# The output projection of a self-attention in three rounded passes, with its weights split on GpSimd

## The chip, the cores and the metric

The kernel runs on one core of a Trainium2 chip. The metric is the device time of one execution in microseconds, the median of several runs. One further execution was recorded by the hardware profiler.

## The reference, cut to what matters

One layer of a perceiver, in fp32, on 256 query tokens of width 512: cross attention to 25088 context rows, self-attention with 16 heads of 64, and a mixture of 32 experts beside a shared expert. The change lies in the last line of the self-attention:

```python
def _L0_attn_ref(x, Wq, bq, Wk, bk, Wv, bv, Wo):
    ...
    attn = jax.nn.softmax(scores, axis=-1)
    out = jnp.einsum('bhqk,bhkd->bhqd', attn, v)
    out = out.transpose(0, 2, 1, 3).reshape(b, n, h * dv)   # 256 x 1024
    return out @ Wo                                          # Wo: 1024 x 512
```

Around it: `x = x + xattn(layernorm(x), ctx)`, `x = x + attn(layernorm(x))`, `x = x + ffn(layernorm(x))`.

## The kernel before

The program is written out by engine, with semaphores between the engines; SyncE (SP) issues all transfers, on one queue.

**Stage one**, to about 583 us, streams the context in 49 blocks of 512 rows. Its matmuls are made in three passes of rounded parts: an operand a is split into a_hi, which is a rounded to the type fp32r, and a_lo = a - a_hi, and the product is a_hi b_hi + a_hi b_lo + a_lo b_hi. ScalarE makes the high parts by a copy, VectorE the low ones by a subtraction. All other matmuls of the kernel have fp32 operands.

**Stage two**, about 583 to 712 us, is the end of the cross attention, then the self-attention. Queries, keys and values of all heads are projected first. The heads come in pairs, c = 0 to 7. For a pair, TensorE makes the scores (`pair_scores`), VectorE the maxima (`head_max`), ScalarE the exponentials (`head_exps`), VectorE scales them by the reciprocal sums (`head_norm`), TensorE transposes them (`head_transposes`), ScalarE copies the transposes out of PSUM (`head_probs_out`), TensorE multiplies them by the values into PSUM bank 4 (`pair_products`), and ScalarE copies that result to SBUF (`pair_out`, tile o_t). TensorE adds the pair's share of the output projection by `output_part(c, t)`, one fp32 matmul of 512 columns for each half t of the tokens. The order on TensorE is written by hand: in turn c it is the scores of pair c+1, the transposes of head 2c, `output_part(c - 2, 0)`, the transposes of head 2c+1, the products of pair c-1, `output_part(c - 2, 1)`. Behind the last turn come the two shares of pair 6, the products of pair 7, eight matmuls that only keep the engine busy, and the two shares of pair 7. VectorE then adds the projection to x (semaphore ao_in_psum), takes the layer norm, and the router follows.

**Stage three** is the experts: a gate, an up and a down tile of 2 MB for each of 32. `load_turn(e, k)` loads tile k (0 gate, 1 up, 2 down) of expert e. The first twelve experts use eight buffers in rotation, `turn_place(e, k)` = (3e + k) mod 8, and a buffer is loaded again when the product that read it is done. The first eight tiles go out in stage two, at points that SP's queue sets by waits: the three tiles of expert 0 after end_products (about 606 us), then the shared expert's weights and w_o, then (1,1) (1,0) (1,2), (2,0) after the products of pair 7 (aot_in_psum), and (2,1) after the projection (ao_in_psum). (2,2) waits for expert 0's gate product. The tile (0,2) lies at RINGB + 5 * WB.

GpSimd makes constants in the first 6 us and has nothing to do after that.

Of the kernel before, what the change touches and what calls it, by code (L numbers as in the profile page):

```python
# [6 lines left out]
F32 = mybir.dt.float32  # L7
F32R = mybir.dt.float32r
BF16 = mybir.dt.bfloat16
I32 = mybir.dt.int32  # L10
ACT = mybir.ActivationFunctionType
ALU = mybir.AluOpType
AX_X = mybir.AxisListType.X

P = 128
D = 512
NQ = 256
NK = 25088
HC = D // P
QT = NQ // P  # L20
# [10 lines left out]
AC = DA // P  # L31
HB = 4
SB = 3
E = 32
FI = 1024
IC = FI // P
# [34 lines left out]
def perceiver_layer(nc, a):  # L71
    with ExitStack() as ctx:

        LOW = 16512
        RINGB = 81888
        WB = D * FI * 4 // P

        def at(name, shape, dt, offset):
            return nc.alloc_sbuf_tensor_at(name, shape, dt, offset=offset)
# [26 lines left out]
        small = cursor[0]  # L106
# [16 lines left out]
        an = at("an", [P, QT, D], F32, small + 8192)  # L123
        a_t = at("a_t", [P, HC, NQ], F32, small + 12288)
        q_t = at("q_t", [P, AC, NQ], F32, small)
        o_t = at("o_t", [P, AC, NQ], F32, small)
        k_t = at("k_t", [P, AC, NQ], F32, small + 24576)
        va = at("va", [P, QT, DA], F32, small + 32768)
        rows = at("rows", [P, 5 * D], F32, small + 40960)
# [63 lines left out]
        o = RINGB + 11 * kb  # L193
        qc_t = at("qc_t", [P, HC, NQ], F32, o)
        kc_t = at("kc_t", [P, HC, NQ], F32, o + 4096)
        o = RINGB + 12 * kb
# [3 lines left out]
        o = RINGB + 13 * kb  # L200
        kq_t = at("kq_t", [P, HC, NQ], F32, o)
        vc = at("vc", [P, QT, D], F32, o + 4096)
        o = RINGB + 12 * kb
# [6 lines left out]
        w_k = at("w_k", [P, HC, DA], F32, RINGB + (2 * 3 + 1) * WB)  # L210
        w_v = at("w_v", [P, HC, DA], F32, RINGB + (2 * 3 + 2) * WB)
        w_o = at("w_o", [P, AC, D], F32, RINGB + 2 * 3 * WB)

        wg_shared = at("wg_shared", [P, HC, FI], F32, RINGB)
        wu_shared = at("wu_shared", [P, HC, FI], F32, RINGB + WB)
# [7 lines left out]
        ps = ctx.enter_context(nc.psum_tensor("ps", [P, 8, 512], F32))  # L223
# [23 lines left out]
        acct_in_psum acct_ready c2s_in_psum c2s_ready c2st_in_psum c2st_ready gate_in_psum z_ready  # L247
        gate_ready an_ready at_in_psum at_ready qa_in_psum qa_ready ka_in_psum ka_ready
        va_in_psum va_ready
        as_in_psum abias_ready aexp_ready aprob_ready apt_in_psum apt_ready aot_in_psum aot_ready ao_in_psum  # L250
        y_ready yt_in_psum yt_ready logits_in_psum maxlog_ready token_scale_ready onehot_ready ranks_in_psum counts_in_psum
        sh_gate_in_psum sh_up_in_psum sh_silu_ready sh_h_ready sh_down_done
        gsel_ready gather_in_psum slotrep_ready slotrow_in_psum slotrow_ready
# [3 lines left out]
        s = {n: ctx.enter_context(nc.semaphore(n)) for n in names}  # L257
# [72 lines left out]
        def _(sp):  # L330
# [80 lines left out]
            def load_turn(e, k):  # L411
                load_tile(e, k, turn_place(e, k))

            sp.wait_ge(s["end_products"], 2 * QT)
            for k in range(3):
                load_turn(0, k)
            sp.dma_start(wd_shared[:, :, :], chunks(a["s_down"])).then_inc(s["dsh_loaded"], 16)
            sp.wait_ge(s["c2s_in_psum"], QT)
# [10 lines left out]
            sp.wait_ge(s["aot_in_psum"], AC)  # L429
            load_turn(2, 0)  # L430
            sp.wait_ge(s["ao_in_psum"], 2)
            load_turn(2, 1)
            for i in range(NR, 3 * NSH):
                e, k = i // 3, i % 3
# [42 lines left out]
        @block.gpsimd  # L477
        def _(pool):
            step = Chain(pool, s["pool_step"])
            step(pool.memset(identb[:, :], 0.0))  # L480
            pool.affine_select(out=identb[:, :], in_=identb[:, :], compare_op=ALU.not_equal, fill=1.0, base=0,
                               pattern=[[-1, P]], channel_multiplier=1).then_inc(s["identb_made"], 1)
            step(pool.memset(ident[:, :], 0.0))
            pool.affine_select(out=ident[:, :], in_=ident[:, :], compare_op=ALU.not_equal, fill=1.0, base=0,
                               pattern=[[-1, P]], channel_multiplier=1).then_inc(s["ident_made"], 1)
            step(pool.memset(maskb[:, :], 0.0))

            step(pool.affine_select(out=maskb[:, :], in_=maskb[:, :], compare_op=ALU.is_ge, fill=MASKED, base=0,
                                    pattern=[[-1, P]], channel_multiplier=1))
            step(pool.memset(ones[:, :], 1.0))  # L490
            step(pool.memset(upper[:, :], 1.0))

            step(pool.affine_select(out=upper[:, :], in_=upper[:, :], compare_op=ALU.is_gt, fill=0.0, base=0,
                                    pattern=[[1, P]], channel_multiplier=-1))
            step(pool.iota(iota32i[:, :], pattern=[[1, SLOT]], base=0, channel_multiplier=0))
            step(pool.tensor_copy(iota32[:, :], iota32i[:, :]))
            for j in range(JG):

                step(pool.iota(slot_tab_i[j * SLOT:(j + 1) * SLOT, :], pattern=[[SLOT, E + OV]], base=0,
                               channel_multiplier=1))  # L500
            pool.tensor_copy(slot_tab[:, :], slot_tab_i[:, :]).then_inc(s["consts_made"], 1)


        @block.tensor
        def _(pe):
            mm = pe.matmul
# [104 lines left out]
            for t in range(QT):  # L611
                for c in range(HC):
                    last = mm(ps[:, 5, t:t + 1], qc_t[:, c, t * P:(t + 1) * P], b_ks[:, c:c + 1],
                              start=(c == 0), stop=(c == HC - 1))
# [3 lines left out]
            for c in range(HC):  # L618
                last = mm(ps[:, 4, 0:NQ], bqs_rep[:, c, :], kc_t[:, c, :], start=(c == 0), stop=(c == HC - 1))
# [13 lines left out]
            for t in range(NSEL // P):  # L633
                for c in range(HC):
                    last = mm(out[:, t, :], sel_t[:, c, t * P:(t + 1) * P], kq_t[:, c, :], start=(c == 0), stop=(c == HC - 1))
# [5 lines left out]
            for t in range(QT):  # L641
                for c in range(HC):
                    last = mm(ps[:, 4 + t, :], c_t[:, c, t * P:(t + 1) * P], w_vc[:, c, :], start=(c == 0), stop=(c == HC - 1))
# [9 lines left out]
            for t in range(QT):  # L653
                for c in range(QT):
                    last = mm(ps[:, 6 + t, :], pavg_t[:, c, t * P:(t + 1) * P], vc[:, c, :], start=(c == 0), stop=(c == QT - 1))
# [120 lines left out]
            for o in range(AC // 2, AC):  # L776
                for c in range(HC):
                    last = mm(by_chunk(2, AC)[:, o, :], w_q[:, c, o * P:(o + 1) * P], a_t[:, c, :],
                              start=(c == 0), stop=(c == HC - 1))
# [27 lines left out]
            def pair_products(c):  # L807

                pe.wait_ge(s["apt_ready"], 2 * c + 2)
                if c:  # L810
                    pe.wait_ge(s["aot_ready"], c)
                heads = [(ps[DK * k:DK * (k + 1), 4, :], 2 * c + k) for k in range(2)]
                for o, h in heads:
                    mm(o[:, 0:NQ], va[:, 0, h * DK:(h + 1) * DK], patt_t[:, h % HB, 0:NQ], start=True, stop=True)
                for o, h in heads:
                    last = mm(o[:, P:NQ], va[:, 1, h * DK:(h + 1) * DK], patt_t[:, h % HB, NQ:NQ + P], start=False, stop=True,
                              skip_group_check=True)
                last.then_inc(s["aot_in_psum"], 1)

            def output_part(c, t):  # L820

                pe.wait_ge(s["aot_ready"], c + 1)
                last = mm(ps[:, 3 + 2 * t, :], o_t[:, c, t * P:(t + 1) * P], w_o[:, c, :], start=(c == 0), stop=(c == AC - 1))
                if c == AC - 1:
                    last.then_inc(s["ao_in_psum"], 1)

# [15 lines left out]
            pair_products(0)  # L842
            values(1, 1)
            pe.wait_ge(s["va_ready"], 4)
            pe.wait_ge(s["wo_loaded"], 16)
            for c in range(2, AC):
                if c + 1 < AC:
                    pair_scores(c + 1)
# [19 lines left out]
            for c in range(HC):  # L868
                for j in range(JG):
                    tokens = y_t[:, c, :].rearrange("p (t j i) -> p t j i", t=QT, j=JG)[:, :, j, :]  # L870
                    last = mm(ps[j * E:(j + 1) * E, 6, 0:QT * SLOT].rearrange("p (t i) -> p t i", t=QT), w_router[:, c, :], tokens,
                              start=(c == 0), stop=(c == HC - 1))
# [161 lines left out]
        def _(act):  # L1034
# [141 lines left out]

            def pair_out(c):
                act.wait_ge(s["aot_in_psum"], c + 1)
                act.activation(o_t[:, c, :], ps[:, 4, 0:NQ], ACT.Copy).then_inc(s["aot_ready"], 1)

            for h in range(2):
                head_exps(h)
# [41 lines left out]
        def _(dve):  # L1224
# [102 lines left out]
            for c in range(HC):  # L1327
                last = dve.tensor_scalar(bqs_rep[:, c, :], ones[:, :], b_qs[:, c:c + 1], None, ALU.mult)
# [118 lines left out]
            def value_rows(n):  # L1447
                dve.wait_ge(s["va_in_psum"], n + 1)
                dve.tensor_tensor(va[:, n // 2, (n % 2) * D:(n % 2 + 1) * D], ps[:, v_bank[n], :],
                                  r_v[:, (n % 2) * D:(n % 2 + 1) * D], ALU.add).then_inc(s["va_ready"], 1)  # L1450
# [31 lines left out]
            def head_norm(h):  # L1482
                m = h % HB
                dve.wait_ge(s["aexp_ready"], h + 1)
                step(dve.reciprocal(arec[m], asum[m]))
                dve.tensor_scalar(patt[:, m, 0:P], patt[:, m, 0:P], arec[m][:, 0:1], None, ALU.mult)
                dve.tensor_scalar(patt[:, m, P:3 * P], patt[:, m, P:3 * P], arec[m][:, 1:2], None, ALU.mult
                                  ).then_inc(s["aprob_ready"], 1)

            for o in range(6):  # L1490
                key_columns(o)
            for h in range(2):
                head_max(h)
            for c in range(AC):
                for h in range(2 * c, 2 * c + 2):
                    head_norm(h)
                if c == 0:
                    for o in range(6, AC):
                        key_columns(o)
                for h in range(2 * c + 2, min(2 * c + 4, NH)):  # L1500
                    head_max(h)
                if c < 2:
                    value_rows(2 + c)
            for t in range(QT):
                dve.wait_ge(s["ao_in_psum"], t + 1)
                step(dve.tensor_tensor(x[:, t, :], x[:, t, :], ps[:, 3 + 2 * t, :], ALU.add))
                row_stats(t)
# [199 lines left out]
```

## Time and profile before

| | |
|---|---|
| median of the runs | 1167.31 us (3 runs, 1166.6 to 1172.64) |
| the profiled execution | 1165.06 us, span 1163.3 us |
| busy share of the span | TensorE 89%, VectorE 53%, ScalarE 32%, GpSimd 0% |
| mean granted clock of TensorE | 0.971 |
| moved by DMA | 381.48 MB, mean 328 GB/s |

Times within the profile count from the first instruction. A busy matmul's end is modelled, since matmuls are pipelined, so distances are read from start to start. "Idle before" an instruction is the idle time of its engine ahead of it, and the arrow names what ended it.

### The profile page before, as it was taken

The numbers are of one execution on the slowest core, as the hardware profiler recorded it, in microseconds if no ns is written. First come the engines' busy times: TensorE is split into PE (matmuls) and PEld (weight loads), VectorE is DVE, ScalarE is ACT, GpSimd is POOL, SyncE is SP. The second block draws the span as 40 slices with busy tenths as digits, with TensorE's granted clock in tenths as the row PEclk, the third lists the DMA queues.
The fourth block names the chain that finished last, engine by engine and source line by source line (L and its number), as shares of the span: only waits on it lengthen the run. The fifth ranks groups of instructions, "written<-read, shape, count | busy, mean of one in ns | idle before, by whom it ended". The sixth has DMA issues, their size and how long they took to land.

```text
span 1163.3 us, 16777 instructions
## 1 busy us (share of the span) xinstructions
PE 1038.4 (89%) x6736; PEld 714.6 (61%) x6736; DVE 618.1 (53%) x977; ACT 372.8 (32%) x546; POOL 3.5 (0%) x20
## 2 busy tenths in 40 slices
PE   9999999999999999999999999999887666667666
PEld 8867878878888888888866756454432222222223
DVE  4457878878878878878854365222121111111112
ACT  2444456546546556546433252000000000000000
POOL 1000000000000000000000000000000000000000
PEclk9999999999999999999999999999997898997989
DMA  9548799887888887888859435999999999999997
GB/s 347 188 145 301 284 350 349 305 297 282 286 296 284 285 303 278 286 298 282 287 193 384 145 145 230 428 425 425 426 426 426 428 428 428 428 428 429 426 429 308
DMA packets 91122, 381.48 MB, mean 328 GB/s; under 512 B 5584, under 2 KB 6224, under 8 KB 74064
## 3 DMA queue, kind: packets, MB, share of 16 engines
q1 hardware_dynamic: 91088, 381.00, 84.1%
q8 instruction: 25, 0.41, 0.1%
q14 instruction: 9, 0.07, 0.0%
HBM read 355.29 MB, written 25.69 MB: 327 GB/s over the span
## 4 chain that ended last, share of the span: by engine, by line
DMA 47%; PE 27%; DVE 17%; SPq 4%; ACT 2%; issue 2%; DVEq 0%; ACTq 0%
DMA deep<-in_r_down 23%; DMA strips<-turned 11%; DMA pt<-strips 9%; DVE nat_lo L1261 4%; DVE turned L1288 4%; PE ps L984 4%; DVE pt_lo L1266 4%; SPq L351 3%; DMA wide<-in_r_up 3%; DVE st L1273 2%; ACT pt_hi L1052 2%; PE ps L544 2%; PE ps L970 2%; PE ps L964 1%; DMA nat<-in_ctx_rows 1%
## 5 line engine op out<-in xcount | busy, mean ns | idle before, releaser
L558 PE MATMUL ps<-ctt_hi,q_hi 128*128 128x512 f32 x392 | 153.7, 392 | 0.0
L560 PE MATMUL ps<-ctt_hi,q_lo 128*128 128x512 f32 x392 | 152.6, 389 | 0.0
L559 PE MATMUL ps<-ctt_lo,q_hi 128*128 128x512 f32 x392 | 152.5, 389 | 0.0
L571 PE MATMUL ps<-nat_hi,pt_hi 128*128 128x512 f32 x368 | 143.8, 391 | 3.9 <-DVE pt_lo L1266 3.9
L573 PE MATMUL ps<-nat_hi,pt_lo 128*128 128x512 f32 x368 | 143.3, 389 | 0.0
L572 PE MATMUL ps<-nat_lo,pt_hi 128*128 128x512 f32 x368 | 143.3, 389 | 0.0
L1205 ACT ACTIVATE sg<-ps 128x256 f32<-128x256 f32 x32 | 12.3, 384 | 388.0 <-PE ps L964 388.0
L1602 DVE TENSOR_TENSOR hh<-sg,ps 128x256 f32<-128x256 f32 x32 | 13.5, 421 | 227.7 <-PE ps L970 227.7
L984 PE MATMUL ps<-deep,hh_t 128*32 128x512 f32 x496 | 77.9, 756 | 54.9 <-DMA deep<-in_r_down 53.6
L1256 DVE TENSOR_TENSOR ctt_lo<-ctt,ctt_hi 128x2048 fp32r<-128x2048 f32 x49 | 111.0, 2289 | 18.6 <-ACT ctt_hi L1044 18.2
L1048 ACT ACTIVATE nat_hi<-nat 128x2048 fp32r<-128x2048 f32 x48 | 92.1, 1918 | 79.4 <-DMA nat<-in_ctx_rows 79.4
L1261 DVE TENSOR_TENSOR nat_lo<-nat,nat_hi 128x2048 fp32r<-128x2048 f32 x48 | 109.9, 2289 | 9.2 <-ACT nat_hi L1048 6.9
L970 PE MATMUL ps<-wide,xg 128*32 128x256 f32 x1024 | 67.3, 407 | 45.3 <-DMA wide<-in_r_up 45.3
L1044 ACT ACTIVATE ctt_hi<-ctt 128x2048 fp32r<-128x2048 f32 x49 | 92.9, 1922 | 30.0 <-DMA ctt<-in_ctx_t 30.0
L1052 ACT ACTIVATE pt_hi<-pt 128x1024 fp32r<-128x1024 f32 x48 | 48.2, 1052 | 135.2 <-DMA pt<-strips 135.2
L1266 DVE TENSOR_TENSOR pt_lo<-pt,pt_hi 128x1024 fp32r<-128x1024 f32 x48 | 56.6, 1222 | 56.0 <-ACT pt_hi L1052 56.0
L558 PEld LDWEIGHTS ps<-ctt_hi,q_hi 128*128 128x128 f32 x392 | 73.6, 188 | 15.6 <-issue 0.5
L559 PEld LDWEIGHTS ps<-ctt_lo,q_hi 128*128 128x128 f32 x392 | 73.6, 188 | 15.6 <-issue 0.5
L560 PEld LDWEIGHTS ps<-ctt_hi,q_lo 128*128 128x128 f32 x392 | 73.6, 188 | 15.3
L571 PEld LDWEIGHTS ps<-nat_hi,pt_hi 128*128 128x128 f32 x368 | 69.1, 188 | 20.6 <-issue 6.4
L970 PEld LDWEIGHTS ps<-wide,xg 128*32 128x32 f32 x1024 | 32.7, 115 | 76.8 <-DMA wide<-in_r_up 55.9
L573 PEld LDWEIGHTS ps<-nat_hi,pt_lo 128*128 128x128 f32 x368 | 69.1, 188 | 14.5
(281 smaller groups left out, 1257.4 us busy)
## 6 DMA issues: line engine op xcount, KB each, us to landing
wide<-in_r_gate SPq DMA_DIRECT2D x32, 2048.0 KB, 26.0
wide<-in_r_up SPq DMA_DIRECT2D x32, 2048.0 KB, 27.4
deep<-in_r_down SPq DMA_DIRECT2D x31, 2048.0 KB, 25.8
ctt<-in_ctx_t SPq DMA_DIRECT2D x49, 1024.0 KB, 7.9
nat<-in_ctx_rows SPq DMA_DIRECT2D x48, 1024.0 KB, 7.4
strips<-turned SPq DMA_DIRECT2D x96, 256.0 KB, 5.1
pt<-strips SPq DMA_DIRECT2D x24, 1024.0 KB, 4.8
w_gate<-in_w_g_t SPq DMA_DIRECT2D x2, 1024.0 KB, 13.6
```

What stands on the lines that cost most here:

```text
L558: mm(o, qh, ctt_hi[par][:, c, :], start=(c == 0), stop=False)
L559: mm(o, qh, ctt_lo[par][:, c, :], start=False, stop=False)
L560: last = mm(o, ql, ctt_hi[par][:, c, :], start=False, stop=(c == HC - 1))
L571: mm(o, p_hi[:, w, :], n_hi[:, t, :], start=(first and t == 0), stop=False)
L572: mm(o, p_hi[:, w, :], n_lo[:, t, :], start=False, stop=False)
L573: last = mm(o, p_lo[:, w, :], n_hi[:, t, :], start=False, stop=(final and t == KT - 1))
L970: last = mm(ps[j * SLOT:(j + 1) * SLOT, 1, 0:GW], xg[:, c, :], up_w[:, c, j * GW:(j + 1) * GW], start=(c == 0), stop=(c == HC - 1))
L984: last = mm(ps[j * SLOT:(j + 1) * SLOT, 3, :], hh_t[:, m, :], down_w[:, m, :], start=(m < JG), stop=(m >= IC - JG))
L1044: act.activation(ctt_hi[par][:, :, :], ctt[par][:, :, :], ACT.Copy).then_inc(s["ctt_hi_ready"], 1)
L1256: dve.tensor_tensor(ctt_lo[par][:, :, :], ctt[par][:, :, :], ctt_hi[par][:, :, :].bitcast(F32), ALU.subtract).then_inc(s["ctt_lo_ready"], 1)
L1261: dve.tensor_tensor(lo[:, :, :], src[:, :, :], hi[:, :, :].bitcast(F32), ALU.subtract).then_inc(s["nat_lo_ready"], 1)
L1266: dve.tensor_tensor(pt_lo[:, half, :, :].rearrange("p w (g i) -> p w g i", g=G), pt[:, :, half, :, :].rearrange("p g w i -> p w g i"), pt_ ...
```

## The change

The attention output and w_o are both split in two rounded parts, and `output_part` makes three matmuls of fp32r for one of fp32. ScalarE's copy `pair_out` now writes the high part o_hi; VectorE makes o_lo from PSUM and o_hi in a new step `out_lo`, between the scalings of the two heads of a later pair. GpSimd makes the parts of w_o in two halves: w_o_hi at the place of tile (0,2), w_o_lo over w_o itself. So tile (0,2), expert 0's down tile, is loaded only after the projection, ahead of (2,1). TensorE waits for both parts of the output before it uses them or writes bank 4 again, and for the half of w_o in question; its single wait for w_o is gone.

```diff
+        o_hi = at("o_hi", [P, AC, NQ], F32R, small)
+        o_lo = at("o_lo", [P, OL, NQ], F32R, small + 40960 + 3 * D * 4)
...
+        w_o_lo = at("w_o_lo", [P, AC, D], F32R, RINGB + 2 * 3 * WB)
+        w_o_hi = at("w_o_hi", [P, AC, D], F32R, RINGB + 5 * WB)
...
             sp.wait_ge(s["end_products"], 2 * QT)
-            for k in range(3):
+            for k in range(2):
                 load_turn(0, k)
...
             sp.wait_ge(s["ao_in_psum"], 2)
+            load_turn(0, 2)
             load_turn(2, 1)
...
+            pool.wait_ge(s["end_products"], 2 * QT)
+            pool.wait_ge(s["wo_loaded"], 16)
+            for h in range(2):
+                part = slice(h * AC // 2, (h + 1) * AC // 2)
+                pool.tensor_copy(w_o_hi[:, part, :], w_o[:, part, :]).then_inc(s["wohi_ready"], 1)
+                pool.wait_ge(s["wohi_ready"], h + 1)
+                pool.tensor_tensor(w_o_lo[:, part, :], w_o[:, part, :], w_o_hi[:, part, :].bitcast(F32),
+                                   ALU.subtract).then_inc(s["wolo_ready"], 1)
...
                 if c:
-                    pe.wait_ge(s["aot_ready"], c)
+                    pe.wait_ge(s["ohi_ready"], c)
+                    pe.wait_ge(s["olo_ready"], c)
...
-                pe.wait_ge(s["aot_ready"], c + 1)
-                last = mm(ps[:, 3 + 2 * t, :], o_t[:, c, t * P:(t + 1) * P], w_o[:, c, :], start=(c == 0), stop=(c == AC - 1))
+                pe.wait_ge(s["ohi_ready"], c + 1)
+                pe.wait_ge(s["olo_ready"], c + 1)
+                pe.wait_ge(s["wolo_ready"], c // (AC // 2) + 1)
+                o, oh, ol = ps[:, 3 + 2 * t, :], o_hi[:, c, t * P:(t + 1) * P], o_lo[:, c % OL, t * P:(t + 1) * P]
+                mm(o, oh, w_o_hi[:, c, :], start=(c == 0), stop=False)
+                mm(o, oh, w_o_lo[:, c, :], start=False, stop=False)
+                last = mm(o, ol, w_o_hi[:, c, :], start=False, stop=(c == AC - 1))
...
-            pe.wait_ge(s["wo_loaded"], 16)
...
-                act.activation(o_t[:, c, :], ps[:, 4, 0:NQ], ACT.Copy).then_inc(s["aot_ready"], 1)
+                act.activation(o_hi[:, c, :], ps[:, 4, 0:NQ], ACT.Copy).then_inc(s["ohi_ready"], 1)
...
+            def out_lo(c):
+                dve.wait_ge(s["ohi_ready"], c + 1)
+                dve.tensor_tensor(o_lo[:, c % OL, :], ps[:, 4, 0:NQ], o_hi[:, c, :].bitcast(F32), ALU.subtract
+                                  ).then_inc(s["olo_ready"], 1)
...
             for c in range(AC):
-                for h in range(2 * c, 2 * c + 2):
-                    head_norm(h)
+                head_norm(2 * c)
+                if c >= 2:
+                    out_lo(c - 2)
+                head_norm(2 * c + 1)
...
+            out_lo(AC - 2)
+            out_lo(AC - 1)
```

## Rows read from the trace of the kernel before

**Rows 1.** The page: DMA busy tenths in 40 slices, and one group of instructions.

```profile
DMA  9548799887888887888859435999999999999997
...
L1602 DVE TENSOR_TENSOR hh<-sg,ps 128x256 f32<-128x256 f32 x32 | 13.5, 421 | 227.7 <-PE ps L970 227.7
```

**Rows 2.** The chain that ended last, in order of time: start, us, what.

```profile
823.05 34.17 DMA wide<-in_r_up
```

**Rows 3.** Windows: length, busy us by engine, clock, DMA share, GB/s.

```profile
715.50:716.00 0.50, 0.50 (x5) 0.49 (x5) 0.43 (x2) 0.00 (x0) 0.00 (x0) 1.00 0.00 0
...
720.50:721.00 0.50, 0.50 (x16) 0.22 (x8) 0.43 (x3) 0.00 (x0) 0.00 (x0) 1.00 1.94 360
...
720.00:760.00 40.00, 38.10 (x375) 20.53 (x368) 15.40 (x54) 1.94 (x6) 0.00 (x0) 1.00 0.99 413
```

**Rows 4.** SP's issues in order of time: start, us, line, transfer.

```profile
606.43 0.43 SPq L409 DMA_DIRECT2D deep<-in_r_down  x1
...
646.69 0.38 SPq L423 DMA_DIRECT2D w_o<-in_w_o  x1
...
703.45 0.33 SPq L409 DMA_DIRECT2D wide<-in_r_gate  x1
705.91 0.33 SPq L409 DMA_DIRECT2D wide<-in_r_up  x1
719.62 0.33 SPq L409 DMA_DIRECT2D deep<-in_r_down  x1
```

**Rows 5.** The timeline of one turn over pairs, and its window.

```profile
679.09 0.49 PE L794 MATMUL ps<-k_t,q_t 64*128 64x128 f32 x4
...
679.31 0.40 ACT L1179 ACTIVATE o_t<-ps 128x256 f32<-128x256 f32 x1
...
679.47 0.17 DVE L1485 RECIPROCAL st<-st 128x2 f32<-128x2 f32 x1
...
679.87 0.35 DVE L1487 TENSOR_SCALAR patt<-patt,st 128x256 f32<-128x256 f32 x1
...
680.40 1.02 PE L823 MATMUL ps<-w_o,o_t 128*128 128x512 f32 x2
...
681.26 0.49 PE L804 MATMUL ps<-ident,patt 128*128 128x128 f32 x3
...
683.76 0.40 ACT L1179 ACTIVATE o_t<-ps 128x256 f32<-128x256 f32 x1
...
679.09:683.54 4.45, 4.45 (x29) 2.35 (x29) 2.90 (x14) 2.86 (x12) 0.00 (x0) 1.00 1.01 429
```

**Rows 6.** The timeline of the score loop, TensorE, two successive matmuls of one kind.

```profile
580.00 0.39 PE L558 MATMUL ps<-ctt_hi,q_hi 128*128 128x512 f32 x1
...
580.68 0.39 PE L558 MATMUL ps<-ctt_hi,q_hi 128*128 128x512 f32 x1
```

**Rows 7.** The timeline of the last pair's projection.

```profile
703.46 0.38 ACT L1179 ACTIVATE o_t<-ps 128x256 f32<-128x256 f32 x1 [3.19 <-PE ps L816]
...
703.89 1.98 PE L823 MATMUL ps<-w_o,o_t 128*128 128x512 f32 x4
...
705.05 0.69 DVE L1506 TENSOR_TENSOR x<-x,ps 128x512 f32<-128x512 f32 x1 [7.02 <-PE ps L823]
```

**Rows 8.** The down tiles of the experts: their matmuls, first and last start.

```profile
L984 PE MATMUL ps<-deep,hh_t x496: 589/617/1062, 724.9 to 1143.4; 128*32 128x512 f32 x166
```

**Rows 9.** The tile w_o: from its issue to its landing.

```profile
DMA to landing us min/median/max: 8.4/8.4/8.4
```

**Rows 10.** GpSimd's timeline: its two casts.

```profile
3.88 0.21 POOL L496 CAST iota<-iota32i 128x32 f32<-128x32 int32 x1
...
5.04 0.22 POOL L501 CAST slot_tab<-slot_tab_i 128x39 f32<-128x39 int32 x1
```

**Rows 11.** The timeline around the first heads: a scaling and the transposes.

```profile
660.08 0.29 DVE L1486 TENSOR_SCALAR patt<-patt,st 128x128 f32<-128x128 f32 x1
...
662.51 0.82 PE L804 MATMUL ps<-ident,patt 128*128 128x128 f32 x6
```

More of the change, by code:

```diff
@@ L33 @@
 SB = 3
+OL = 4
 E = 32
@@ L125, in perceiver_layer @@
         q_t = at("q_t", [P, AC, NQ], F32, small)
-        o_t = at("o_t", [P, AC, NQ], F32, small)
+        o_hi = at("o_hi", [P, AC, NQ], F32R, small)
+        o_lo = at("o_lo", [P, OL, NQ], F32R, small + 40960 + 3 * D * 4)
         k_t = at("k_t", [P, AC, NQ], F32, small + 24576)
@@ L249, in perceiver_layer @@
         va_in_psum va_ready
-        as_in_psum abias_ready aexp_ready aprob_ready apt_in_psum apt_ready aot_in_psum aot_ready ao_in_psum
+        as_in_psum abias_ready aexp_ready aprob_ready apt_in_psum apt_ready aot_in_psum ohi_ready olo_ready wohi_ready wolo_ready ao_in_psum
         y_ready yt_in_psum yt_ready logits_in_psum maxlog_ready token_scale_ready onehot_ready ranks_in_psum counts_in_psum
```

## The prediction

> **What bounds the kernel now.** I read the page first: its slices show the DMA engines busy at nine tenths and more over the last two fifths of the span, at some 426 GB/s [rows 1]. The chain that ended last says how that hangs together with the engines: up to 823.05 us it runs through TensorE's work, from there it is expert tiles, beginning with one that takes 34.17 us in a full queue [rows 2]. So I asked the windows where that stream of tiles begins. In 720 to 760 us the share is 0.99 already, with the ramp inside [rows 3]. The issue list names what starts it: the down tile of expert 2 goes out at 719.62 us, when expert 0's gate product is done, and packets flow from 720.5 us [rows 3, 4]. It and the tiles behind it are 88 (96 less the eight issued before) of 2 MB, 4.9 us each at 426 GB/s, 431 us. The end is therefore the moment of that issue plus a fixed sum. What is done before 720 us counts by how much it moves that moment, and by whether it leaves the DMA engines more bytes behind it.
>
> Before that moment the DMA engines are partly empty. Expert 2's gate and up tiles, issued at 703.45 and 705.91 us, are through before 715.5 us (0 GB/s in 715.5 to 716.0) [rows 3, 4]. The hole is 5 us wide.
>
> **The projection's matmuls.** Each of the 16 calls of output_part is now one fp32 matmul, recorded as two instructions; the next work starts 0.86 us behind its start (680.40 to 681.26) [rows 5]. The shape that replaces it (128x128 stationary, 512 columns, fp32r, three of them) is in the score loop: one of a kind starts at 580.00 us and the next of its kind at 580.68, so 0.68 us for three, with the weight loads under them [rows 6]. That is 0.18 us less for a call, 2.9 us for all 16, if TensorE were alone.
>
> **The loop over pairs.** One turn lasts 4.45 us (679.09 to 683.54), all of it TensorE [rows 5]. With two calls shorter by 0.18 TensorE would need 4.09. But VectorE gets a new link. Now ScalarE copies a pair's output out of PSUM (start 679.31, 0.40), and the projection waits for that alone. After the change VectorE takes the low part behind it, between the scalings of two heads. It is a 128x256 operation with one operand in PSUM, and the nearest row has 421 ns [rows 1]. I follow the turn. Call its start S (679.09). The copy starts at S+0.22 now; in a shorter turn it falls at S+0.40, as it hangs on the odd head's transposes of the turn before, 2.50 us ahead of it (681.26 to 683.76, with a copy and the exponentials of two heads between) [rows 5]. Those transposes stand at S+2.17 now and at S+1.99 with the shorter call, and 1.99 + 2.50 - 4.09 is 0.40. Copy to S+0.80, low part from S+0.83, its result at S+1.25 (TensorE reaches the first projection call at S+1.31, 680.40). VectorE can start the next independent operation 0.35 after the low part's start, and the odd head's reciprocal and two scalings take 0.75 (679.47 to 679.87 + 0.35), so they end at S+1.93, and its transposes want them at S+1.99. The ring copy, low part, odd scaling, transposes, exponentials, copy is 0.40+0.03+0.35+0.75+0.05+2.50 = 4.08 us. So TensorE's 4.09 and the ring's 4.08 meet, and I take 4.15, as three waits now lie within 0.06 us of each other: 0.30 less for each of the five turns from 674.63 to 696.9. Bounds: 0.36 each (TensorE alone) and 0. Sum: -1.5 us (-1.8 to 0).
>
> VectorE's own work grows from 2.90 to 3.3 us of a turn [rows 5], so it does not become the bound. The maxima of the next two heads come 0.7 us later; they are needed only after the odd head's transposes and their copy.
>
> **Behind the loop.** Turn 7 has no scores, so TensorE is not ahead there: the low part stands before head 15's scaling and costs 0.16 at its transposes. The two calls for pair 6 then wait 0.22 for its low part, and gain 0.36. For pair 7 the copy starts at 703.46 and the projection at 703.89 [rows 7]; the low part puts 0.42 more between, so the last calls start 0.30 later than they would otherwise, with eight short matmuls as the only cover. VectorE's addition at 705.05 [rows 7] waits for the first of the last two calls, which is 0.18 shorter. Added up, this part loses 0.1 us against its place now (-0.2 to +0.5). Together -1.4 us at the addition, and the layer norm, router, gather and expert 0's gate behind it are a plain chain, so the issue at 719.62 moves by as much.
>
> **The moved tile.** 2 MB leave the queue at 606.43 us and enter it behind the projection, between expert 2's gate and up tiles [rows 4]. Nothing on TensorE waits for the transfers that come earlier thereby (the shared weights, used after 712 us). In its new place: the first of three is issued at 703.45 less 1.6 (it waits for the last pair product, not for the low part), two tiles take at most 12.05 from there as now, the third 4.9: through at 718.8 at the latest. The stream restarts at 720.5 - 1.4 = 719.1. It fits the hole with 0.3 or more to spare, so I cost it at nothing; if the hole were gone it would cost 4.9. Expert 0's down product starts at 724.9 [rows 8], and its tile, second in the queue, is there at about 714, some 9 us ahead.
>
> **GpSimd's four instructions.** w_o is issued at 646.69 and lands after 8.4 us, at 655.1 [rows 4, 9]. The trace has no GpSimd instruction of 2048 elements. Casts of 39 and of 32 columns take 0.22 and 0.21 us, 1.4 ns a column, which gives 2.9 us more, 3.1 us for each; rounding of the last digit leaves this anywhere from 0 to 2.9 ns a column, so up to 6.1 us [rows 10]. At 3.1 the four end at about 667.6 us, the first half at 661.4. The first half is first used in the turn before the one shown, at 675.9, the second half four turns later: hidden with 14 us, and even at 6.1 us each (667.3 and 679.5).
>
> What they may do to VectorE is the open term. Heads 0 and 1 are scaled from 660.08 to 661.44, in the middle of the first subtraction, and TensorE transposes them from 662.5 [rows 11]. There is slack of 1.0 us. If VectorE waits once for the rest of one GpSimd instruction (to 661.4), head 0 is ready at 662.0 and head 1 at 662.8, and nothing is lost. If GpSimd and VectorE took turns, instruction by instruction, head 1 could be ready as late as 667.6 + 0.7 = 668.3, where TensorE takes it at 662.9 now: +5.4 us, straight onto the chain. Bounds 0 and 5.4; no row shows the two engines contending, so I take 0.
>
> These scalings read and write SBUF at 0.5 ns a column: 128 more columns add 0.06 us (0.29 at 660.08 to 0.35 at 679.87) [rows 5, 11]. The Trainium skill (SBUF — State Buffer, section Who interferes with whom) says that GpSimd and a VectorE operation in a two-port mode share one pair of ports under an exclusive lock held for a whole instruction, which speaks against this change. Its GPSIMD Engine Reference (section Performance versus the Vector engine) gives 4497 ns for a two-input operation of 2048 elements; by that, an estimate, GpSimd would be at work until about 669 us and meet heads 2 and 3 too, and the sum would come out at or above zero. No row here shows such a lock.
>
> **Sum.** The profiled execution took 1165.06 us, 1163.3 of it span. -1.5 + 0.1 + 0 + 0 = -1.4: 1163.7. The median of the runs is 1167.31, 2.25 above the profiled one, so 1165.9 in the runs' terms.
>
> **The rivals.**
> 1. The scalings wait for GpSimd. Place: heads 0 and 1 at 660 us, heads 2 and 3 at 667.6. For it: the two-wide rows; against it: the slack of 1.0. Price by the rows: the four instructions end at 658.2, 661.4, 664.5 and 667.6; once around for head 1 it is ready at 664.5 + 0.8 = 665.3 instead of 662.9 when TensorE would take it, +2.4; the worst +5.4. From a wait of 1.4 on the chain the kernel is slower. Time: 1167.31 - 1.4 + 2.4 = 1168.3, up to 1171.3. The locking rule of the skill is this rival; in its terms the price would be near 2 to 6 us.
> 2. The ring gives everything back: out_lo behind ScalarE's copy holds the odd head's scaling longer than I read, and the turn stays at 4.4. Then 1167.31 + 0.1 - 0.3 = about 1167.1. For it: three waits within 0.06 us; against: it needs 0.3 us in each turn.
> 3. The moved tile is not hidden: the engines are still on it when the stream could restart. For it: only 0.3 us spare that is sure; against: the hole is plain in the windows. If half of it stuck out, +2.5 - 1.4: 1168.4; all of it, 1170.8.
> 4. The change does not reach the end at all because the stream is full. Against: the stream starts with an issue that waits for TensorE. It gives 1167.3.
>
> **How the numbers follow.** Forecast 0.45; rival 1 0.28; rival 2 0.10; rival 3 0.08; rival 4 0.03; something not seen 0.06. The forecast's own range is 1164.8 to 1167.2. The measured medians scatter too (1166.6 to 1172.64 in three runs), so 8 in 10 is 1163.5 to 1171.5: below are TensorE's full 2.9 us and a low median, above the worst of rival 1. Half a per cent is 5.8 us, about what such a measurement can tell from nothing. Faster by more than that needs 4.4 us that no row offers: 0.04. Slower needs 7.2 us of new waits: 0.07. The same: 0.89.
>
> **What would show it.** The projection's line with 48 records and 0.68 us a call; turns of 4.1 to 4.2 us; a VectorE operation of about 0.42 us behind each ScalarE copy; the GpSimd instructions over by 668 us (longer, or scalings of more than 0.35 us, or TensorE idle before head transposes at 662 to 669 us, is rival 1); expert 2's down tile issued near 718.2 us; a DMA hole of under 1 us in front of it. Wrong would be: that issue at 719.6 or later, a turn of 4.4, or no hole and the stream's start behind the issue.

## The result: slower by two thirds of a per cent

Over 20 runs of each, the changed kernel took 1175.60 us in the median (1170.3 to 1184.89) and the kernel before 1168.21 us (1162.11 to 1172.64). The ratio is 1.0067, 95% interval 1.0052 to 1.0082. The forecast was 1.4 us less than before, and the kernel takes 7.4 us more: 1175.60 us lies 4.1 above the upper end of the range, 1171.5. Slower by more than half a per cent had been given 0.07. What happened is rival 1, at a price above the worst that I had worked out for it.

The profiled execution of the changed kernel took 1176.97 us, span 1175.2, against 1165.06 and 1163.3. Of these 11.9 us, 4.07 lie ahead of everything that the change touches: expert 0's gate tile is issued at 609.63 us, and was at 605.56. Between executions that moment moves by as much as 10 us without any change (605.6 to 615.2 us in the profiles of this study), while what lies behind the stretch moves by 2.4 us. By these profiles it is most of the scatter of the runs. So profiles are best compared by a stretch that leaves it out, and I use one throughout: **from the issue of expert 0's gate tile to the issue of expert 2's down tile**, the one that starts the stream of tiles. It was 114.06 us (605.56 to 719.62, [rows 4]) and is 120.86 us. SP's issues in the changed kernel, start and duration:

```profile
609.63 0.35 SPq L413 DMA_DIRECT2D wide<-in_r_gate  x1
...
713.98 0.33 SPq L413 DMA_DIRECT2D wide<-in_r_gate  x1
716.60 0.33 SPq L413 DMA_DIRECT2D deep<-in_r_down  x1
716.97 0.44 SPq L413 DMA_DIRECT2D wide<-in_r_up  x1
730.49 0.33 SPq L413 DMA_DIRECT2D deep<-in_r_down  x1
```

The stretch, from one profile of each kernel, gives +6.80 of the 7.39 us between the medians. Where it is lost is in GpSimd's and VectorE's timelines of the changed kernel, from 659 us (4.07 later than the same place in [rows 11]):

```profile
659.04 1.90 POOL L512 CAST w_o_hi<-w_o 128x2048 fp32r<-128x2048 f32 x1 [653.80 <-DMA w_o<-in_w_o]
661.02 4.51 POOL L514 TENSOR_TENSOR w_o_lo<-w_o,w_o_hi 128x2048 fp32r<-128x2048 f32 x1
665.47 1.89 POOL L512 CAST w_o_hi<-w_o 128x2048 fp32r<-128x2048 f32 x1
667.44 4.49 POOL L514 TENSOR_TENSOR w_o_lo<-w_o,w_o_hi 128x2048 fp32r<-128x2048 f32 x1
```

```profile
661.13 0.88 DVE L1491 TENSOR_SCALAR k_t<-ps,cols 128x256 f32<-128x256 f32 x2 [2.58 <-PE ps L777]
...
662.35 0.41 DVE L1498 TENSOR_REDUCE st<-ps 128x1 f32<-128x256 f32 x1
662.80 2.75 DVE L1499 TENSOR_SCALAR st<-st 128x2 f32<-128x2 f32 x1
...
666.11 1.27 DVE L1499 TENSOR_SCALAR st<-st 128x2 f32<-128x2 f32 x1
...
667.48 4.53 DVE L1505 TENSOR_SCALAR patt<-patt,st 128x128 f32<-128x128 f32 x1
```

An operation on two numbers a partition takes 2.75 us, where its like takes 0.17 when GpSimd rests. It ends at 665.55, when GpSimd's first subtraction ends (665.53). The next of its kind takes 1.27 and ends at 667.38, with the second rounding (667.36). The first scaling takes 4.53 instead of 0.29 and ends at 672.01, with the second subtraction (671.93). The operations that read PSUM, in the same stretch, take what they always take: 0.41 for the maximum over 256 columns and 0.88 for the two of keys. The profile books this waiting as busy time of VectorE, not as idle time with a releaser: on VectorE the long duration is the only sign of it.

TensorE's side, the changed kernel:

```profile
666.64 0.49 PE L808 MATMUL ps<-k_t,q_t 64*128 64x128 f32 x4 [0.97 <-ACT patt L1189]
...
672.33 1.56 PE L818 MATMUL ps<-ident,patt 128*128 128x128 f32 x6 [4.55 <-DVE patt L1506]
673.69 4.49 PE L771 MATMUL ps<-w_v,a_t 128*128 128x512 f32 x8
678.11 0.49 PE L808 MATMUL ps<-k_t,q_t 64*128 64x128 f32 x4
```

Against the kernel before, each counted from expert 0's gate tile: the scores of pair 1 are 1.04 us late (their waits hang on the exponentials, these on the two small operations), the first transposes 5.75, the scores of pair 2 7.34. The last 1.6 have two parts. From the start of the transposes to that of the value product it is 1.36 us instead of 0.66: head 1's scalings end 0.66 us behind head 0's, and TensorE now waits for them. And the value product takes 4.49 us instead of 3.60. The windows (columns as in [rows 3]) show why it does:

```profile
667.80:672.30 4.50, 0.00 (x0) 0.00 (x0) 4.50 (x3) 0.53 (x3) 4.13 (x1) 0.59 0.90 386
672.30:678.00 5.70, 5.67 (x14) 2.86 (x14) 2.77 (x11) 2.70 (x10) 0.00 (x0) 0.72 0.03 10
```

TensorE did nothing for 4.5 us and its granted clock fell (0.59 of full speed as a mean of that stretch and 0.72 behind it, so part of both at the lower level of 1.2 GHz; 1.00, which is 2.4 GHz, again from 678 us).

From pair 2's scores on, the gains come in, but small ones. From the scores of pair 3 to the issue of expert 2's down tile it is 44.45 us (686.04 to 730.49) instead of 44.99: 0.54 gained where 1.4 was forecast. A turn lasts 4.23 us. Here is one, all engines:

```profile
694.78 0.40 ACT L1198 ACTIVATE o_hi<-ps 128x256 fp32r<-128x256 f32 x1
695.22 0.43 DVE L1511 TENSOR_TENSOR o_lo<-ps,o_hi 128x256 fp32r<-128x256 f32 x1 [0.33 <-ACT o_hi L1198]
...
695.75 0.47 PE L841 MATMUL ps<-w_o_hi,o_hi 128*128 128x512 f32 x1
...
696.52 0.49 PE L818 MATMUL ps<-ident,patt 128*128 128x128 f32 x3
...
697.05 0.49 ACT L1194 ACTIVATE patt_t<-ps 128x384 f32<-128x384 f32 x1 [0.64 <-PE ps L818]
...
699.02 0.40 ACT L1198 ACTIVATE o_hi<-ps 128x256 fp32r<-128x256 f32 x1
```

The low part ends at 695.65 and the first pass of the projection starts 0.10 later, although this pass reads only high parts: TensorE waits for both parts ahead of the first of three matmuls.

### The profile page after: what moved, and what is told of

It reads as the page before. It is cut to its first block, busy times and chain, and to the rows that moved or that the text cites. A ratio compares the mean times of both kernels' runs of the same rounds, so it can differ in the third digit from the quotient of the medians.

```text
span 1175.2 us, 16838 instructions
## 1 busy us (share of the span) xinstructions
PE 1038.6 (88%) x6752; PEld 720.2 (61%) x6752; DVE 628.2 (53%) x985; ACT 373.1 (32%) x546; POOL 16.2 (1%) x24
## 4 chain that ended last, share of the span: by engine, by line
DMA 47%; PE 27%; DVE 18%; SPq 3%; ACT 2%; issue 2%; DVEq 0%; ACTq 0%
DMA wide<-in_r_up 17%; DMA strips<-turned 11%; DMA pt<-strips 9%; DMA deep<-in_r_down 9%; DVE nat_lo L1280 4%; DVE pt_lo L1285 4%; DVE turned L1307 4%; SPq L355 3%; PE ps L989 3%; PE ps L1003 2%; DVE st L1292 2%; ACT pt_hi L1071 2%; PE ps L558 2%; PE ps L983 1%; PE ps L545 1%
```

## The experiments

Seven more kernels ran. In each the stretch defined above is read from one profile; five were also timed against the kernel before, and two ran once. The intervals are some 0.2% to either side, 2 to 3 us: they tell a loss of 7 us from nothing, but not a gain of 1 or 2.

| kernel | stretch, us | ratio to before, 95% interval |
|---|---|---|
| before | 114.06 | 1 |
| changed | 120.86 | 1.0067 (1.0052 to 1.0082) |
| tile_late | 114.04 | 0.9981 (0.9960 to 1.0001) |
| pool_alone | 121.52 | 1.0060 (1.0037 to 1.0082) |
| gpsimd_early | 113.50 | 0.9994 (0.9972 to 1.0016) |
| early_latewait | 112.17 | 1.0002 (0.9978 to 1.0027) |
| pieces | 114.21 | 1.0010 (0.9990 to 1.0030) |
| warm_wait | 119.68 | one execution, 1173.09 us |
| gpsimd_gate | 121.93 | one execution, 1180.67 us |

### The moved tile alone

The kernel before, with only expert 0's down tile moved.

```diff
-            for k in range(3):
+            for k in range(2):
                 load_turn(0, k)
...
             sp.wait_ge(s["ao_in_psum"], 2)
+            load_turn(0, 2)
             load_turn(2, 1)
```

> The kernel before with the moved tile alone: expert 0's down tile is issued behind the projection, nothing else changed. My measure is the stretch from the issue of expert 0's gate tile to the issue of expert 2's down tile, which is 114.06 us before (605.56 to 719.62) and 120.86 after (609.63 to 730.49). Theory A (the move is hidden, as forecast): the stretch stays at 114.1 us within 0.2, the DMA hole ahead of the stream shrinks from 5 us to under 1, and the time is that of before within 0.3%. Rival (the tile sticks out of the hole or the stream loses its start): the stretch is the same but the end comes 2 to 5 us later, ratio 1.002 to 1.004.

The stretch stayed, 114.04 us, and the ratio is 0.9981 with an interval that holds 1. The hole ahead of the stream (columns as in [rows 3]) shrank to part of one slice of half a microsecond; expert 2's down tile is issued at 720.85 us here:

```profile
720.50:721.00 0.50, 0.50 (x16) 0.28 (x12) 0.41 (x3) 0.14 (x1) 0.00 (x0) 1.00 0.92 393
721.00:721.50 0.50, 0.50 (x18) 0.29 (x12) 0.41 (x3) 0.24 (x1) 0.00 (x0) 1.00 0.24 98
721.50:722.00 0.50, 0.50 (x16) 0.33 (x12) 0.43 (x3) 0.00 (x0) 0.00 (x0) 1.00 2.27 426
```

The tile is hidden, with nothing to spare. Rival 3 is out as the cause.

### GpSimd's four instructions alone

The same, with GpSimd's work. The projection is that of the kernel before and does not read what GpSimd makes; the subtraction therefore writes over w_o_hi, and SP waits for it before it loads tile (0,2) there.

```diff
+            pool.wait_ge(s["end_products"], 2 * QT)
+            pool.wait_ge(s["wo_loaded"], 16)
+            for h in range(2):
+                part = slice(h * AC // 2, (h + 1) * AC // 2)
+                pool.tensor_copy(w_o_hi[:, part, :], w_o[:, part, :]).then_inc(s["wohi_ready"], 1)
+                pool.wait_ge(s["wohi_ready"], h + 1)
+                pool.tensor_tensor(w_o_hi[:, part, :], w_o[:, part, :], w_o_hi[:, part, :].bitcast(F32),
+                                   ALU.subtract).then_inc(s["wolo_ready"], 1)
```

> The kernel before with the moved tile and GpSimd's four instructions; the projection keeps its single fp32 matmul, and what GpSimd makes is not used. Theory A (the loss is VectorE waiting for GpSimd, instruction by instruction): the stretch from expert 0's gate tile to expert 2's down tile grows from 114.1 to 121.3 or 121.5 us (+7.3: 1.0 at the scores of pair 1, 4.7 more at the transposes of head 0, 0.9 from matmuls at half clock behind it, the rest between), VectorE operations that read and write SBUF last as long as the GpSimd instruction beside them, and the ratio is 1.006 to 1.008. Rival B (the loss is in the three passes and their new waits): the stretch stays at 114.1 to 114.6 and the ratio is 1.000.

The stretch is 121.52 us, +7.46 against 114.06, and the ratio 1.0060: the whole loss, and a little more, without a single new matmul, new VectorE operation or new wait of TensorE. VectorE's and TensorE's rows repeat those of the changed kernel:

```profile
664.78 2.80 DVE L1492 TENSOR_SCALAR st<-st 128x2 f32<-128x2 f32 x1
...
668.14 1.27 DVE L1492 TENSOR_SCALAR st<-st 128x2 f32<-128x2 f32 x1
...
669.51 4.54 DVE L1498 TENSOR_SCALAR patt<-patt,st 128x128 f32<-128x128 f32 x1
```

```profile
674.37 1.56 PE L816 MATMUL ps<-ident,patt 128*128 128x128 f32 x6 [4.55 <-DVE patt L1499]
675.72 4.58 PE L769 MATMUL ps<-w_v,a_t 128*128 128x512 f32 x8
```

Rival B, the passes and their waits, is out.

### The changed kernel, with GpSimd's work where VectorE rests

VectorE has nothing for 17 us while TensorE makes queries and keys. For GpSimd to work there, w_o must be there earlier; it takes the shared down tile's place and turn, and expert 2's up tile takes w_o's.

```diff
-        w_o = at("w_o", [P, AC, D], F32, RINGB + 2 * 3 * WB)
-        w_o_lo = at("w_o_lo", [P, AC, D], F32R, RINGB + 2 * 3 * WB)
+        w_o = at("w_o", [P, AC, D], F32, RINGB + 2 * WB)
+        w_o_lo = at("w_o_lo", [P, AC, D], F32R, RINGB + 2 * WB)
...
-            sp.dma_start(wd_shared[:, :, :], chunks(a["s_down"])).then_inc(s["dsh_loaded"], 16)
+            sp.dma_start(w_o[:, :, :], chunks(a["w_o"])).then_inc(s["wo_loaded"], 16)
...
-            sp.dma_start(w_o[:, :, :], chunks(a["w_o"])).then_inc(s["wo_loaded"], 16)
+            load_turn(2, 1)
...
             load_turn(0, 2)
-            load_turn(2, 1)
+            sp.dma_start(wd_shared[:, :, :], chunks(a["s_down"])).then_inc(s["dsh_loaded"], 16)
...
             pool.wait_ge(s["wo_loaded"], 16)
+            pool.wait_ge(s["va_ready"], 2)
```

> The changed kernel with GpSimd's work moved to where VectorE is idle: w_o is loaded early into the place of the shared expert's down tile, GpSimd starts when VectorE has made its second value tile (it then has nothing for 17 us), the shared down tile comes behind the projection and expert 2's up tile comes at the place of w_o's load. The bytes behind the projection are as in the changed kernel. Theory A (lock by GpSimd is the loss): no VectorE operation longer than in the kernel before, GpSimd over before the first maxima, stretch 114.06 - 0.9 + 0.3 = 113.2 to 113.6 us, ratio to before 0.998 to 1.001. Rival B (three passes and their waits lose it): stretch near 120.9, ratio 1.006.

The stretch is 113.50 us: 7.36 less than in the changed kernel, and 0.56 less than before. The ratio is 0.9994 (0.9972 to 1.0016), so the loss is gone; a gain of 0.56 us is too small for the runs to show. The same four instructions take the same time and stand between two rows of VectorE that are 17.29 us apart:

```profile
642.62 1.89 POOL L513 CAST w_o_hi<-w_o 128x2048 fp32r<-128x2048 f32 x1 [637.38 <-DVE va L1469]
...
651.03 4.52 POOL L515 TENSOR_TENSOR w_o_lo<-w_o,w_o_hi 128x2048 fp32r<-128x2048 f32 x1
```

```profile
641.76 0.69 DVE L1469 TENSOR_TENSOR va<-ps,rows 128x512 f32<-128x512 f32 x1 [0.70 <-PE ps L772]
659.74 0.88 DVE L1492 TENSOR_SCALAR k_t<-ps,cols 128x256 f32<-128x256 f32 x2 [17.29 <-PE ps L778]
```

### The same, with the wait for the low part moved

```diff
                 pe.wait_ge(s["ohi_ready"], c + 1)
-                pe.wait_ge(s["olo_ready"], c + 1)
                 pe.wait_ge(s["wolo_ready"], c // (AC // 2) + 1)
...
                 mm(o, oh, w_o_lo[:, c, :], start=False, stop=False)
+                pe.wait_ge(s["olo_ready"], c + 1)
                 last = mm(o, ol, w_o_hi[:, c, :], start=False, stop=(c == AC - 1))
```

> As the previous one, and TensorE waits for the low part of the attention output only ahead of the third pass, not ahead of the first. In the changed kernel a turn over pairs is 4.23 us (690.18, 694.41, 698.64, 702.87). Theory A (the ring is ScalarE's copy, VectorE's low part, the first projection call, the odd head's transposes, ScalarE: 0.40+0.04+0.43+0.07+0.77+0.03+2.50 = 4.24, so TensorE's early wait sets it): turns of 4.09 to 4.12, last calls 0.4 us earlier, stretch 1.1 us shorter than in the previous kernel, about 112.3. Rival B (VectorE's order, the low part between the two scalings, sets it): turns stay at 4.2. Ratio to before 0.996 to 0.999.

Turns fell from 4.23 to 4.13 us, just outside the 4.09 to 4.12 expected, and the stretch by 1.33 to 112.17, a little more than expected. Two turns of TensorE:

```profile
675.37 0.49 PE L809 MATMUL ps<-k_t,q_t 64*128 64x128 f32 x4 [0.78 <-DVE va L1469]
...
679.50 0.49 PE L809 MATMUL ps<-k_t,q_t 64*128 64x128 f32 x4
...
683.63 0.49 PE L809 MATMUL ps<-k_t,q_t 64*128 64x128 f32 x4
```

So the early wait did set the turn. But the time did not follow: the ratio is 1.0002 (0.9978 to 1.0027), above the 0.996 to 0.999 that I expected, though the interval reaches down to 0.998: 1.3 us less is 0.1% of the time, and the runs cannot show whether it is there. The windows, with expert 2's down tile issued at 718.48 us, show what may stand in the way:

```profile
718.50:719.00 0.50, 0.50 (x16) 0.33 (x12) 0.43 (x3) 0.37 (x1) 0.00 (x0) 1.00 1.05 385
719.00:719.50 0.50, 0.50 (x16) 0.27 (x10) 0.40 (x4) 0.00 (x0) 0.00 (x0) 1.00 1.14 397
```

There is no hole left at the issue: the engines are still on the moved tiles, so a shorter stretch may no longer start the stream sooner. That such a gain is lost to the moved tile is argued from these rows, not shown; no kernel separated it from the scatter.

### GpSimd's work in small pieces, at its old place

```diff
-            for h in range(2):
-                part = slice(h * AC // 2, (h + 1) * AC // 2)
...
+            for i in range(2 * AC):
+                c, part = i // 2, slice(i % 2 * D // 2, (i % 2 + 1) * D // 2)
...
-                pe.wait_ge(s["wolo_ready"], c // (AC // 2) + 1)
+                pe.wait_ge(s["wolo_ready"], 2 * c + 2)
```

> The changed kernel with GpSimd's four instructions of 2048 columns cut into 32 of 256. Theory A (a VectorE operation waits for the end of the GpSimd instruction that it meets): no VectorE operation of this stretch is held longer than one piece, some 0.7 us, instead of 2.75, 1.27 and 4.53 us; the stretch from expert 0's gate tile to expert 2's down tile falls from 120.86 to 114 to 116 us. Rival (the two engines share by bandwidth, or VectorE waits until GpSimd has nothing left): the waits add up to the same, stretch 119 to 121.

The stretch is 114.21 us, 6.65 less than with four long instructions, and the ratio 1.0010 (0.9990 to 1.0030). GpSimd is at work for 18.4 us here, 5.5 longer, and meets more of VectorE's operations, but each waits only for the piece at hand:

```profile
665.15 0.40 POOL L512 CAST w_o_hi<-w_o 128x256 fp32r<-128x256 f32 x1
665.63 0.73 POOL L514 TENSOR_TENSOR w_o_lo<-w_o,w_o_hi 128x256 fp32r<-128x256 f32 x1
...
666.77 0.73 POOL L514 TENSOR_TENSOR w_o_lo<-w_o,w_o_hi 128x256 fp32r<-128x256 f32 x1
```

```profile
665.61 0.83 DVE L1505 TENSOR_SCALAR patt<-patt,st 128x128 f32<-128x128 f32 x1
...
666.76 0.15 DVE L1504 RECIPROCAL st<-st 128x2 f32<-128x2 f32 x1
666.95 0.63 DVE L1505 TENSOR_SCALAR patt<-patt,st 128x128 f32<-128x128 f32 x1
```

Scalings last 0.83 and 0.63 instead of 0.29, and end with the piece beside them (666.44 and 666.36; 667.58 and 667.50). The reciprocal between them keeps its 0.15. This is waiting by whole instruction. Shared bandwidth would not make the scalings end with the pieces, and the rival built on it expected 119 to 121 us.

### TensorE kept busy through its wait

```diff
             def head_transposes(h):
+                if h == 0:
+                    keep_warm(72, 3)
                 pe.wait_ge(s["aprob_ready"], h + 1)
```

> The changed kernel with 72 small matmuls (about 4.2 us) that keep TensorE busy while it waits for the first head's scaling. Theory A (0.9 us of the loss is the value product at the lower clock behind the idle stretch: 4.49 us instead of 3.60): granted clock 1.00 from 660 to 680 us, that product at 3.6 us, the stretch 0.9 us shorter than in the changed kernel, 119.9 to 120.1. Rival (it is slow for another reason, such as w_v or PSUM): the stretch stays at 120.9.

The stretch is 119.68 us, 1.18 less than in the changed kernel and so a little more than the 0.9 expected. The value product has its 3.60 us again (0.9), and it starts 1.04 us behind the transposes instead of 1.36 (0.3):

```profile
663.76 4.18 PE L525 MATMUL ps<-identb 128*128 128x128 bf16 x72
668.49 1.21 PE L820 MATMUL ps<-ident,patt 128*128 128x128 f32 x6 [0.55 <-DVE patt L1508]
669.53 3.60 PE L771 MATMUL ps<-w_v,a_t 128*128 128x512 f32 x8
```

The granted clock is 1.00 in all of 660 to 680 us. So of the 7.3 us, 1.2 are a clock that fell while TensorE stood idle, by one profile of each kernel; the rest is the waiting itself.

### GpSimd's work beside other kinds of VectorE's operations

The kernel with the early start, without the line `pool.wait_ge(s["va_ready"], 2)`.

> The kernel with GpSimd's early start, without its wait for the value tiles: it starts as soon as w_o is there, some 15 us behind the issue of expert 0's gate tile, in the middle of the gate and layer norm of the cross attention, where VectorE has operations with two inputs in SBUF, one-input operations in SBUF, statistics, and operations from PSUM. Theory A (VectorE is held in every operation that needs SBUF for both an input and more, two inputs or the fast one-input form, and not in those from PSUM): the subtraction, the multiplication and the addition of 512 columns (0.69 us) or the normalisation (0.55 us) that meet a GpSimd instruction last until its end, up to 4.5 us; the stretch grows from 113.5 to 119 or more. Rival (only the fast one-input form is held): the two-input ones keep 0.69 us and the stretch grows by under 5.

w_o landed 19.4 us behind the gate tile's issue, later than expected, so GpSimd met only the second half of the gate. The stretch is 121.93 us, 8.43 longer. GpSimd's and VectorE's rows:

```profile
633.64 4.90 POOL L514 TENSOR_TENSOR w_o_lo<-w_o,w_o_hi 128x2048 fp32r<-128x2048 f32 x1
638.48 2.35 POOL L512 CAST w_o_hi<-w_o 128x2048 fp32r<-128x2048 f32 x1
640.91 4.52 POOL L514 TENSOR_TENSOR w_o_lo<-w_o,w_o_hi 128x2048 fp32r<-128x2048 f32 x1
```

```profile
633.48 0.69 DVE L1462 TENSOR_TENSOR c2s<-c2s,gate 128x512 f32<-128x512 f32 x1 [0.69 <-ACT gate L1162]
634.21 4.88 DVE L1463 TENSOR_TENSOR x<-x,c2s 128x512 f32<-128x512 f32 x1
639.12 0.69 DVE L1248 BATCH_NORM_STATS2 st<-x 128x6 f32<-128x512 f32 x1
...
641.11 4.61 DVE L1268 TENSOR_SCALAR an<-x,st 128x512 f32<-128x512 f32 x1
```

The addition of two SBUF tiles is held 4.2 us (4.88 against 0.69), the normalisation 4.1 (4.61 against 0.55); the statistics, one input in SBUF beside a rounding that runs, keep their 0.69. And it goes both ways: GpSimd's subtraction takes 4.90 where VectorE's multiplication was on its way, its rounding 2.35 where the addition was, instead of 4.5 and 1.9. The two holds add up to 8.25 of the 8.43 us. The rival, only one-input operations held, is out.

## Why the prediction was wrong

**What bounds the kernel: right.** The end is the issue of expert 2's down tile plus a fixed sum. From that issue to the end of the span it was 443.7 us before and 443.7 to 446.1 in the others, a scatter of 2.4 us that the runs do not explain.

**The step that failed: "no row shows the two engines contending, so I take 0".** The absence of a row was taken for a price. The term measured +7.46 us in pool_alone, where it stands almost alone (the moved tile gives -0.02); in the changed kernel it is +7.34 at the scores of pair 2. The scalings had been picked out as the operations at risk, and the page that the prediction cites against the change had it right. The Trainium skill (SBUF — State Buffer, section Who interferes with whom) states the exclusive lock for a whole instruction, for VectorE's two-port modes and for its operations with two inputs in SBUF, and that the engine that comes first has it. The trace agrees: the held operations on two numbers and on 128 columns end 0.02 to 0.08 us behind GpSimd's instruction, the two of 512 columns 0.55 and 0.29 us behind it, and GpSimd's own waits lie beside operations of VectorE that were begun before it.

**My upper bound of the same term, 5.4 us, was also too low**, for three reasons. GpSimd's instructions were mis-sized one by one: 3.1 us each was taken, and 1.9 for a rounding and 4.5 for a subtraction were measured; only their sum was right (12.4 taken, 12.9 measured). The Trainium skill (GPSIMD Engine Reference, section Performance versus the Vector engine) has 4497 ns for a two-input operation of that size; it took 4.51 us here. The estimate that the prediction makes of it, GpSimd at work until about 669 us, needs roundings of some 2.5 us, which it does not state; with its own 3.1 it is 670.3, and 667.9 was measured (671.93 less the 4.07 us that this execution is late). I looked only at the scalings and not at the operations of two numbers ahead of them, which make the bias of the exponentials: these were held 2.6 and 1.1 us, and everything queued behind them on VectorE with them, so that the first scaling met the second subtraction and not the first. And the clock, 1.2 us, was not in the sum at all. The slack of 1.0 us was used up before the scalings began: the first started 3.3 us later than before.

**Three passes for one: right in size, nearly.** A call directly behind another takes 0.70 us. In a turn the call between transposes takes 0.78 instead of 0.86 and the one behind the products 0.89 instead of 1.05, and where the low part is not in the way (early_latewait) the turn is 0.32 us shorter, for 0.36 forecast.

**The loop: mis-sized, by a wait that I passed over.** 4.15 us a turn was taken, 4.23 measured. The ring that I added up went through VectorE's scaling; the longer one goes through TensorE, whose first projection pass waits for the low part: 0.40 + 0.04 + 0.43 + 0.10 + 0.77 + 0.53 + 1.97 = 4.24 us from copy to copy. I had noted that the first call would come 0.06 us behind the low part and let that pass as slack. early_latewait measures the mistake, 0.10 us a turn.

**Behind the loop: mis-sized.** From pair 3's scores to expert 2's down tile 0.54 us were gained instead of 1.4. Up to the transposes of head 14, the end of the loop, 1.04 were gained instead of 1.5, so what follows lost 0.50 where 0.1 was taken. The last projection calls, at 714.93 us, start 0.94 us behind ScalarE's copy instead of 0.43, as they wait for the low part. early_latewait gained 1.33 us, of which the loop explains 0.4; its last calls start 0.44 us behind the copy.

**The moved tile: right.** Hidden, by less than a us (tile_late). **GpSimd off the critical path by its own results: right**, its first half was ready at 665.5 us and first used at 687.3. That is what made the change look harmless: its results were early and its cost lay in another engine's operations.

## What to carry to other kernels

Before work is given to an idle GpSimd, list what VectorE does in that time. In these traces a tensor_scalar from SBUF to SBUF of 2 to 512 columns (only the one of a single column kept its 0.15 us) and an addition of two SBUF tiles waited for the end of the GpSimd instruction that they met; operations from PSUM, reciprocals and statistics did not. The two-input case rests on one row of one run. Put the work where VectorE rests or only has operations of the second kind, or cut it into pieces; the same work cost 7.4 us of the stretch at one place and nothing at another. What is left of the change then is a stretch 0.6 to 1.9 us shorter and no gain that the runs can show. In a profile look for such waiting among the durations, not among the idle times, and when splitting an operand put each wait in front of the pass that needs it.

## What the hardware showed that I had not expected

An operation on 128x2 elements was held 2.6 us. A VectorE operation can also hold GpSimd (2.35 us for a rounding of 1.9). 4.5 us of idleness brought TensorE's granted clock to a mean of 0.59 in that stretch and 0.72 in the 5.7 us behind it, in a kernel that had run at 0.99 to 1.00 from 40 to 609 us; 72 tiny matmuls in the gap kept it at 1.00.
